# Graph and LSTM kernel on one core: the gates' biases go in through PSUM on ScalarE instead of out through VectorE

## The chip, the cores and the metric

The kernel runs on one core of one Trainium2 chip. The metric is the device time of one execution in microseconds, as a median of several runs.

## The reference

There are 6250 nodes with 512 features and 100000 edges sorted by destination. Two layers follow each other, each with a residual sum:

```python
def gnn(x, edge_index, W1, b1, W2, b2):
    agg = jax.ops.segment_sum(x[src], dst, num_segments=N_NODES)
    h = jax.nn.relu((x + agg) @ W1 + b1)
    return jax.nn.relu(h @ W2 + b2)

def step(carry, x_t):            # LSTM over the 6250 nodes, hidden size 512
    combined = jnp.concatenate((x_t, h_prev), axis=1)
    f, i, o = (sigmoid(combined @ W + b) for f, i, o)
    c_t = f * c_prev + i * jnp.tanh(combined @ W_c + b_c)
    h_t = o * jnp.tanh(c_t)

x = x + gnn(layernorm(x), edges, ...)
x = x + lstm(layernorm(x)[None], ...)[0]
```

## The kernel before

The program has three parts, one after another with a barrier between them. The first (`table_part`) makes the table layernorm(x) @ W1. The second (`graph_part`, the graph stage, where the change is) goes over 50 blocks of 125 nodes. The third (`lstm_part`) solves the recurrence over 125 lanes in rounds of 50 steps; it begins by reading `gate_rows`, which the graph stage has stored, and it runs further rounds only if a check of the values asks for them.

The order of work is written by hand, engine by engine, with semaphores between the engines. In the graph stage one iteration `one(i)` mixes the work of three blocks:

- *Columns of block i.* The edges of a block come as 16 columns of 128 edges (`COLUMNS`), some blocks have more ("beyond"). For each column GpSimd gathers 128 rows of the table by indirect DMA. ScalarE copies them to the rounded fp32r array `high` (`high_part`, L875), VectorE subtracts to get the rest (`low_of_rows`, L1045), and TensorE multiplies both by a one-hot matrix (`visit`, L928) and adds into `agg`. `high` and `low_part` are rings of 8, `onehot` too, and are freed by `s_visit`, in fours.
- *Layers of block i-1.* VectorE adds `agg` to the rows' own table rows (`hin`, L1086), TensorE turns them ("the turn of hin", L943), ScalarE applies bias and relu (L887) and rounds (L892), TensorE multiplies by W2 (`late`, L977 and L981), VectorE adds the bias and the residual and takes the statistics, ScalarE normalises (`z`, L902 to L906), and TensorE turns z ("the turn of z", again L943). ScalarE takes the turned rows as `zT.high` (L910), VectorE the rest as `zT.low` (L1060).
- *Gates.* For each block four PSUM banks `gps` of 512 columns get the products of zT with Wx (L949): `gate_high(n)` is 8 matmuls on zT.high, `gate_low(n)` 4 on zT.low. Banks 1 and 0 of block i-1 are computed at the end of iteration i, banks 3 and 2 of block i-2 during iteration i.
- *Banks out.* VectorE's `gate_biases(b, n)` (L1066) adds the bias row `bgr` to the finished bank and writes `gout`, from where SyncE stores it in `gate_rows`.

"Beyond" columns have a conditional path on every engine: GpSimd's `gather_beyond`, ScalarE's `high_beyond` (L881), VectorE's `beyond_columns` (L1052, L1055) and TensorE's `visit_beyond` (L937), the last between `gate_high(1)` and `gate_high(0)`. ScalarE and VectorE do it at the end of the iteration, ahead of the first columns of the next one. After the last iteration ScalarE alone copies three pieces of weights for the LSTM (L919) before it comes to the barrier.

VectorE and TensorE have two iterations unrolled in a loop; ScalarE has one.

Of the kernel before, what the change touches and what calls it, by code (L numbers as in the profile page):

```python
# [33 lines left out]
ALU = mybir.AluOpType  # L34
ACT = mybir.ActivationFunctionType
# [115 lines left out]
SPREAD = 2 * 16  # L151
# [446 lines left out]
def graph_part(nc, x, edges, table, x1_rows, gate_rows, Wx, W2s, b1c, b2r, bgr, s_w, WEIGHTS_LOADED,  # L598
# [21 lines left out]
    L = LANES  # L620
    BANKS = G4 // PAIR

    with ExitStack() as ctx:
# [70 lines left out]
        s_gps = {n: sem(ctx, f"s_gps{n}") for n in (1, 2)}  # L694
        s_gout = [sem(ctx, f"s_gout{n}") for n in range(BANKS)]
        s_x1_st = sem(ctx, "s_x1_st")
        s_g_st = [sem(ctx, f"s_g_st{n}") for n in range(BANKS)]
# [3 lines left out]
        def wait(e, semaphore, value):  # L701

            if not isinstance(value, int) or value > 0:
                e.wait_ge(semaphore, value)
# [50 lines left out]

        CHECKED = 5
        VISITS = COLUMNS // HOTS

# [112 lines left out]
        def _(e):  # L871
# [11 lines left out]
            def first_layer(i):  # L883
# [5 lines left out]
                for half in range(2):  # L889
                    e.wait_ge(s_relu, i * 4 - (2 - 2 * half))  # L890
                    of = slice(2 * half, 2 * half + 2)
                    e.activation(h1T.high[:, of, :], between_T[:, of, :], ACT.Copy).then_inc(s_h1, 1)  # L892

            def one(i, tiles, layers, gates):
                some, beyond = columns_of(i, high_part, beyond_of(e, high_beyond)) if tiles else (no_columns, no_columns)
                some(0, 8)
                if layers:
                    first_layer(i)
                some(8, 15)
                if layers:  # L900
                    e.wait_ge(s_var, i)
                    e.activation(root[0:L, :], ve[0:L, :], ACT.Sqrt).then_inc(s_norm, 1)  # L902
                    e.activation(z[0:L, :], x1[0:L, :], ACT.Identity, bias=minus[0:L, :]).then_inc(s_norm, 1)
                    e.wait_ge(s_norm, i * 4 - 2)
                    e.wait_ge(s_rs, i)
                    e.activation(z[0:L, :], z[0:L, :], ACT.Copy, scale=rs[0:L, :]).then_inc(s_norm, 1)  # L906
                some(15, 16)
                if layers:
                    e.wait_ge(s_turned, i * 2)
                    e.activation(zT.high[:, :, :], rows_turned[:, :, :], ACT.Copy).then_inc(s_norm, 1)  # L910
                beyond()

            e.wait_ge(s_w, WEIGHTS_LOADED)
            all_iterations(e, one)
            e.wait_ge(s_wh, 16 * WH_LOADS // 2)
# [6 lines left out]
        def _(e):  # L922
# [32 lines left out]
            def gate_high(b, n, agg_done=False):  # L955


                wait(e, s_gout[n], b)
                e.wait_ge(s_norm, (b + 1) * 4)
                products = bank_products(n, zT.high, Wx.high, begins=True)  # L960
                if agg_done:
                    products[0].then_inc(s_agg, 1)
                bank_products(n, zT.high, Wx.low)
# [64 lines left out]
        def _(e):  # L1028
# [33 lines left out]

            def gate_biases(b, n):
                wait(e, s_g_st[n], b * SPREAD)
                e.wait_ge(s_gps[1 if n < 2 else 2], b + 1)
                e.tensor_tensor(gout[0:L, n // 2, n % 2, :], gps[n][0:L, :], bgr[0:L, n, :],  # L1066
                                ALU.add).then_inc(s_gout[n], 1)

            def one(i, par, tiles, layers, gates):
# [23 lines left out]
                lows(8, 10)  # L1093
                if gates:
                    gate_biases(i - 2, 0)
                    gate_biases(i - 2, 1)
                if layers:
# [24 lines left out]
                if layers:  # L1122
                    low_of_turned(zT, rows_turned, i)
                if gates:
                    gate_biases(i - 2, 3)
                    gate_biases(i - 2, 2)
                beyond()
# [976 lines left out]
```

## Time and profile before

| | us |
|---|---|
| median of 3 runs | 2652.29 |
| lowest and highest | 2648.72, 2652.97 |
| the profiled execution, its own time | 2650.73 |
| its span, first to last instruction | 2649.1 |
| graph stage, first column to the barrier | 189 to 1360 |

The profile is of one execution. The span is 1.6 us shorter than that execution's own time. "PE" is TensorE's matmuls, "PEld" its weight loads; a matmul's row is longer than the distance to the next one, since they are pipelined, so a wait is seen better in the weight loads. In a timeline row the first number is the start, the second the length, and the bracket at the end is the idle time before it with the releaser.

### The profile page before, as it was taken

Reading aid. Unit: us, or ns where it says so; the run is one execution under the profiler, and the core shown is the slowest. Engines: PE = TensorE matmul, PEld = TensorE weight load, DVE = VectorE, ACT = ScalarE, POOL = GpSimd, SP = SyncE. Lnnn points to the kernel's source line nnn. Section 1 sums busy time; section 2 is a strip of 40 time slices with the busy share of each in tenths; the row PEclk is TensorE's granted clock in tenths of the full one; section 3 lists DMA queues with packets and bytes.
Section 4 is the critical chain, followed back from the end, with each engine's and each line's share of the span. In section 5 each row is a group of like instructions: output and inputs, shape, how many; then the busy total and the mean of one; then the engine's idle time right before and its main releaser. Section 6 shows DMA issues by size and latency. Waiting matters only on the chain. (4 is left out here: it accounts for less than half of the span.)

```text
span 2649.1 us, 47626 instructions
## 1 busy us (share of the span) xinstructions
PE 2505.1 (95%) x10745; PEld 1819.0 (69%) x10746; DVE 2163.1 (82%) x5780; ACT 1561.6 (59%) x3989; POOL 996.0 (38%) x1017
## 2 busy tenths in 40 slices
PE   7978999999999999999979999999998999989997
PEld 6865777777777777777756666666665555555554
DVE  7757888888888888888848887777777888878887
ACT  5645555555555555555536656666665777757775
POOL 1127777777777767777520000000000000023333
PEclk9987999999999999999989999999999999999999
DMA  9647988888888888888777647777778666589996
GB/s 251 188 132 234 293 281 261 263 279 255 276 265 268 266 244 279 275 255 264 238 195 207 192 124 235 237 240 239 237 235 220 173 172 173 142 224 252 252 251 160
DMA packets 194255, 611.12 MB, mean 231 GB/s; under 512 B 41810, under 2 KB 47954, under 8 KB 164444
## 3 DMA queue, kind: packets, MB, share of 16 engines
q1 hardware_dynamic: 120562, 370.34, 47.1%
q0 software_dynamic: 73632, 240.13, 31.4%
q8 instruction: 19, 0.31, 0.0%
q14 instruction: 42, 0.34, 0.0%
HBM read 468.71 MB, written 141.62 MB: 230 GB/s over the span
## 5 line engine op out<-in xcount | busy, mean ns | idle before, releaser
L834 POOL DMA_INDIRECT kept<-ln_table,kept x800 | 822.3, 1028 | 292.0 <-issue 208.2
L1557 PE MATMUL acc<-shared,state 128*125 128x512 f32 x2244 | 799.3, 429 | 14.4 <-ACT state L1434 13.2
L875 ACT ACTIVATE shared<-kept 128x512 fp32r<-128x512 f32 x800 | 442.6, 625 | 157.3 <-PE agg L928 105.4
L1557 PEld LDWEIGHTS acc<-shared,state 128*125 128x125 f32 x2244 | 413.2, 189 | 153.7 <-ACT acc L1486 27.5
L1391 POOL TENSOR_TENSOR out<-h,lx 125x512 f32<-125x512 f32 x50 | 64.4, 1287 | 1102.2 <-DVE h L1903 1102.2
L928 PE MATMUL agg<-shared,onehot 128*125 128x512 f32 x1200 | 377.6, 408 | 20.7 <-DVE shared L1045 18.6
L1557 PE MATMUL acc<-W_low,state 128*125 128x512 f32 x800 | 316.3, 395 | 0.0
L1557 PE MATMUL acc<-last_high,state 128*125 128x512 f32 x748 | 303.6, 406 | 0.0
L928 PEld LDWEIGHTS agg<-shared,onehot 128*125 128x125 f32 x1200 | 225.2, 189 | 97.9 <-DVE low_part L1045 15.7
L1045 DVE TENSOR_TENSOR low_part<-kept,shared 128x512 fp32r<-128x512 f32 x400 | 265.6, 693 | 11.0 <-ACT shared L875 4.4
L1045 DVE TENSOR_TENSOR shared<-kept,shared 128x512 fp32r<-128x512 f32 x400 | 259.5, 688 | 16.9 <-ACT shared L875 11.1
L949 PE MATMUL gps<-Wx_high,zT_high 128*125 128x512 f32 x800 | 224.2, 402 | 0.8 <-ACT zT_high L910 0.8
L949 PE MATMUL gps<-Wx_low,zT_high 128*125 128x512 f32 x800 | 218.8, 395 | 0.0
L1452 ACT ACTIVATE gate<-acc 125x512 f32<-125x512 f32 x200 | 119.8, 599 | 155.7 <-PE acc L1557 154.9
L949 PE MATMUL gps<-Wx_high,zT_low 128*125 128x512 f32 x800 | 209.6, 394 | 0.0
L1478 ACT ACTIVATE tc<-c 125x128 f32<-125x128 f32 x600 | 153.7, 303 | 77.3 <-DVE c L1895 77.0
L887 ACT ACTIVATE between<-rows_turned,b1c 128x125 f32<-128x125 f32 x200 | 56.7, 367 | 218.3 <-PE rows_turned L943 218.3
L1885 DVE TENSOR_TENSOR c<-gate,c 125x256 f32<-125x256 f32 x300 | 126.4, 421 | 72.0 <-ACT gate L1452 70.2
L949 PEld LDWEIGHTS gps<-Wx_low,zT_high 128*125 128x125 f32 x800 | 149.5, 187 | 37.6
L949 PEld LDWEIGHTS gps<-Wx_high,zT_low 128*125 128x125 f32 x800 | 147.9, 185 | 37.9
L1557 PEld LDWEIGHTS acc<-last_high,state 128*125 128x125 f32 x748 | 138.2, 185 | 50.5 <-DVE state L1878 15.4
L1557 PEld LDWEIGHTS acc<-W_low,state 128*125 128x125 f32 x800 | 150.3, 188 | 30.8
(237 smaller groups left out, 4408.9 us busy)
## 6 DMA issues: line engine op xcount, KB each, us to landing
xg<-total_rows SPq DMA_DIRECT2D x100, 896.0 KB
xg<-gate_rows SPq DMA_DIRECT2D x88, 896.0 KB
gate_rows<-gout SPq DMA_DIRECT2D x200, 224.0 KB
total_rows<-total SPq DMA_DIRECT2D x50, 896.0 KB
kept<-ln_table,kept POOLq DMA_INDIRECT x800, 4.5
lx<-x_rows POOLq DMA_DIRECT2D x50, 250.0 KB, 7.4
out_dram<-out POOLq DMA_DIRECT2D x49, 250.0 KB, 2.8
held<-in_x_dram SPq DMA_DIRECT2D x25, 448.0 KB
```

What stands on the lines that cost most here:

```text
L834: e.indirect_dma_start(out=rows[j % RING][:, :], out_offset=None, in_=table[:, :], in_offset=bass.IndirectOffsetOnAxis(ap=ends[:, b, j, 0: ...
L875: e.activation(high[j % PARTS][:, :], rows[j % RING][:, :], ACT.Copy).then_inc(s_high, 1)
L887: e.activation(between_T[:, m, :], rows_turned[:, m, :], ACT.Relu, bias=b1c[:, m:m + 1]).then_inc(s_relu, 1)
L928: m = e.matmul(sums[0:L, :], onehot[:, j % HOT_RING, :], part[j % PARTS][:, :], start=(j == 0 and part is high), stop=(part is low_part), ...
L949: products.append(e.matmul(gps[n][0:L, :], state[:, k, :], weights[:, k, n // 2, n % 2].rearrange("p s c -> p (s c)"), start=(begins and k ...
L1045: e.tensor_tensor(low_part[j % PARTS][:, :], rows[j % RING][:, :], high[j % PARTS][:, :].bitcast(F32), ALU.subtract).then_inc(s_low, 1)
L1391: e.tensor_tensor(out[par][0:L, :], h[par][0:L].rearrange("c k u -> c (k u)"), x1[par][0:L, :], ALU.add).then_inc(s_out, 1)
L1452: e.activation(gates[0:L, half, 0].rearrange("c s u -> c (s u)"), sums, ACT.Sigmoid).then_inc(s_fi[half], 1)
L1478: e.activation(cell_turned[0:L, k], cell[0:L, k], ACT.Tanh).then_inc(s_tc[k], 1)
L1557: m = e.matmul(acc[n][0:L, :], stationary[:, k, :], weights[k][:, n * PAIR:(n + 1) * PAIR], start=begins, stop=(k == K - 1), skip_group_ch ...
L1885: e.tensor_tensor(half_of(cell, half), gates[0:L, half, 0, 0].rearrange("c (k u) -> c k u", k=KH), half_of(cell, half), ALU.mult).then_inc ...
```

## The change

ScalarE writes each bank's bias into PSUM before the block's products (`seed_bank`), TensorE's first product no longer begins the bank anew (`begins=True` is gone) and adds to what is there, and ScalarE copies the finished bank out (`gate_out`) and seeds it again. VectorE's four sums per block are gone. TensorE now waits for the seed (`s_bias`) where it waited for the bank to be read (`s_gout`).

```diff
+        s_bias = [sem(ctx, f"s_bias{half}") for half in range(2)]
...
+        SEEDED_AS = {1: 1, 0: 2, 3: 1, 2: 2}
...
+            def seed_bank(n):
+                e.activation(gps[n][0:L, :], bgr[0:L, n, :], ACT.Copy).then_inc(s_bias[n // 2], 1)
+
+            def gate_out(b, n):
+                wait(e, s_g_st[n], b * SPREAD)
+                e.wait_ge(s_gps[1 if n < 2 else 2], b + 1)
+                e.activation(gout[0:L, n // 2, n % 2, :], gps[n][0:L, :], ACT.Copy).then_inc(s_gout[n], 1)
+                e.wait_ge(s_gout[n], b + 1)
+                seed_bank(n)
...
-                some(8, 15)
+                some(8, 11)
+                if gates:
+                    gate_out(i - 2, 1)
+                    gate_out(i - 2, 0)
+                some(11, 15)
...
                     e.activation(zT.high[:, :, :], rows_turned[:, :, :], ACT.Copy).then_inc(s_norm, 1)
+                if gates:
+                    gate_out(i - 2, 3)
+                    gate_out(i - 2, 2)
                 beyond()
 
             e.wait_ge(s_w, WEIGHTS_LOADED)
+            for n in (1, 0, 3, 2):
+                seed_bank(n)
...
-                wait(e, s_gout[n], b)
+                e.wait_ge(s_bias[n // 2], b * 2 + SEEDED_AS[n])
                 e.wait_ge(s_norm, (b + 1) * 4)
-                products = bank_products(n, zT.high, Wx.high, begins=True)
+                products = bank_products(n, zT.high, Wx.high)
...
-            def gate_biases(b, n):
-                wait(e, s_g_st[n], b * SPREAD)
-                e.wait_ge(s_gps[1 if n < 2 else 2], b + 1)
-                e.tensor_tensor(gout[0:L, n // 2, n % 2, :], gps[n][0:L, :], bgr[0:L, n, :],
-                                ALU.add).then_inc(s_gout[n], 1)
-
...
                 lows(8, 10)
-                if gates:
-                    gate_biases(i - 2, 0)
-                    gate_biases(i - 2, 1)
                 if layers:
                     e.wait_ge(s_late, i)
...
                     low_of_turned(zT, rows_turned, i)
-                if gates:
-                    gate_biases(i - 2, 3)
-                    gate_biases(i - 2, 2)
                 beyond()
```

Three places show what moves. First, ScalarE at the end of an iteration of the loop, from the last column of a block (`rows15`) over `zT.high` to the conditional path of the beyond column. Before:

```order
L875 ACTIVATE shared<-kept 128x512 [waits s_visit,s_rows15]
L910 ACTIVATE zT_high<-rows_turned 128x500 [waits s_rows_turned]
L739 ISA
L739 TENSOR_LOAD ranges
L768 COMPARE_AND_BRANCH
L751 ISA
```

And now, with line numbers of the changed kernel (its L877 is L875 of before, L926 is L910):

```order
L877 ACTIVATE shared<-kept 128x512 [waits s_visit,s_rows15]
L926 ACTIVATE zT_high<-rows_turned 128x500 [waits s_rows_turned]
L902 ACTIVATE gout<-gps 125x512 [waits s_gps2,s_g_st3]
L897 ACTIVATE gps<-bgr 125x512 [waits s_gout3]
L902 ACTIVATE gout<-gps 125x512 [waits s_gps2,s_g_st2]
L897 ACTIVATE gps<-bgr 125x512 [waits s_gout2]
L740 ISA
L740 TENSOR_LOAD ranges
L770 COMPARE_AND_BRANCH
```

Four instructions stand between `zT.high` and everything that follows: the beyond column and the first columns of the next block. Each seed waits for the copy just ahead of it on the same engine.

Second, VectorE before the change at the same place, between the rest of z and the next block's first one-hot (rows of the beyond path left out behind the first two):

```order
L1045 TENSOR_TENSOR low_part<-kept,shared 128x512 [waits s_high] x3
L1060 TENSOR_TENSOR zT_low<-rows_turned,zT_high 128x500 [waits s_norm]
L1066 TENSOR_TENSOR gout<-gps,bgr 125x512 [waits s_gps2,s_g_st3]
L1066 TENSOR_TENSOR gout<-gps,bgr 125x512 [waits s_gps2,s_g_st2]
L739 TENSOR_LOAD ranges
L768 COMPARE_AND_BRANCH
```

The two L1066 are gone there, and the two that stood ahead of the sum on `late` (L1099) are gone as well; nothing takes their place.

Third, ScalarE at the end of the graph stage. Before, `zT.high` of the last block is followed by the weights' copies:

```order
L906 ACTIVATE between<-between,grs 125x512 [waits s_grs,s_norm]
L910 ACTIVATE zT_high<-rows_turned 128x500 [waits s_rows_turned]
L919 ACTIVATE shared<-kept 128x2048 [waits s_visit,s_wh_rest,s_wh]
L919 ACTIVATE shared<-kept 128x2048 x2
L623 UNCONDITIONAL_BRANCH
```

And now:

```order
L902 ACTIVATE gout<-gps 125x512 [waits s_gps2,s_g_st3]
L897 ACTIVATE gps<-bgr 125x512 [waits s_gout3]
L902 ACTIVATE gout<-gps 125x512 [waits s_gps2,s_g_st2]
L897 ACTIVATE gps<-bgr 125x512 [waits s_gout2]
L940 ACTIVATE shared<-kept 128x2048 [waits s_visit,s_wh_rest,s_wh]
L940 ACTIVATE shared<-kept 128x2048 x2
```

The three copies of the weights now stand behind the last bank's copy, which waits for the last product of the stage.

## Rows read from the trace of the kernel before

**Rows 1.** The page, part 1: TensorE, us, share of the span, instructions.

```profile
PE 2505.1 (95%) x10745; PEld 1819.0 (69%) x10746; DVE 2163.1 (82%) x5780; ACT 1561.6 (59%) x3989; POOL 996.0 (38%) x1017
```

**Rows 2.** Busy time by stretch, 300 to 1300 us: busy us of each engine.

```profile
300.00:1300.00 1000.00, 997.67 (x4418) 777.73 (x4417) 891.52 (x1733) 550.79 (x1152) 738.23 (x719) 1.00 0.86 266
```

**Rows 3.** Waits from 300 to 1300 us: total us, times, longest.

```profile
ACT shared L875 <- PE agg L928: 97.5, 44, 2.2
...
PEld rows_turned L943 <- ACT between L906: 19.4, 44, 0.5
...
PEld agg L928 <- DVE low_part L1045: 11.1, 44, 0.4
DVE between L1099 <- PE late L981: 10.3, 42, 0.3
...
PEld rows_turned L943 <- DVE hin L1086: 6.9, 22, 0.4
```

**Rows 4.** Timeline from 700 us, an even iteration, turn of z to turn of hin.

```profile
709.27 0.41 PEld L943 LDWEIGHTS rows_turned<-ident,between 125*128 125x128 f32 x4 [0.44 <-ACT between L906]
...
709.96 0.59 ACT L910 ACTIVATE zT_high<-rows_turned 128x500 fp32r<-128x500 f32 x1 [0.21 <-PE rows_turned L943]
...
710.58 0.68 DVE L1060 TENSOR_TENSOR zT_low<-rows_turned,zT_high 128x500 fp32r<-128x500 f32 x1
...
710.90 4.28 ACT L875 ACTIVATE shared<-kept 128x512 fp32r<-128x512 f32 x8 [0.36 <-issue]
...
713.65 2.49 DVE L1045 TENSOR_TENSOR shared<-kept,shared 128x512 fp32r<-128x512 f32 x4
...
717.95 0.68 DVE L1086 TENSOR_TENSOR hin<-agg,hin 125x512 f32<-125x512 f32 x1
...
718.82 0.59 PEld L943 LDWEIGHTS rows_turned<-ident,hin 125*128 125x128 f32 x4
```

**Rows 5.** Timeline from 685 us, an odd iteration, same stretch.

```profile
686.54 0.41 PEld L943 LDWEIGHTS rows_turned<-ident,between 125*128 125x128 f32 x4 [0.44 <-ACT between L906]
...
691.34 2.53 DVE L1045 TENSOR_TENSOR shared<-kept,shared 128x512 fp32r<-128x512 f32 x4
...
696.38 0.41 PEld L943 LDWEIGHTS rows_turned<-ident,hin 125*128 125x128 f32 x4 [0.36 <-DVE hin L1086]
```

**Rows 6.** ScalarE's line L881 by source, then a timeline from 409 us, a beyond column.

```profile
L881 ACT ACTIVATE high_x<-rows_x x7: 632/632/635, 416.1 to 1279.1; 128x512 fp32r<-128x512 f32 x7
...
413.99 0.41 PEld L943 LDWEIGHTS rows_turned<-ident,between 125*128 125x128 f32 x4 [0.43 <-ACT between L906]
...
416.07 0.63 ACT L881 ACTIVATE high_x<-rows_x 128x512 fp32r<-128x512 f32 x1 [0.81 <-issue]
...
417.33 0.68 DVE L1055 TENSOR_TENSOR low_x<-rows_x,high_x 128x512 fp32r<-128x512 f32 x1
...
418.16 0.47 PE L937 MATMUL agg<-high_x,onehot_x 128*125 128x512 f32 x1 [0.26 <-DVE low_x L1055]
```

**Rows 7.** Groups by line: count, busy us, mean ns, idle before.

```profile
L1452 ACT ACTIVATE gate<-acc 125x512 f32<-125x512 f32 x200 | 119.8, 599 | 155.7 <-PE acc L1557 154.9
L1486 ACT ACTIVATE acc<-xg 125x512 f32<-125x512 f32 x196 | 116.4, 594 | 0.0
...
L1066 DVE TENSOR_TENSOR gout<-gps,bgr 125x512 f32<-125x512 f32 x176 | 112.5, 680 | 0.0
```

**Rows 8.** Timeline from 1335 us, the end of the graph stage.

```profile
1341.90 5.50 ACT L919 ACTIVATE shared<-kept 128x2048 fp32r<-128x2048 f32 x3
...
1355.19 1.29 DVE L1066 TENSOR_TENSOR gout<-gps,bgr 125x512 f32<-125x512 f32 x2 [4.29 <-PE gps L949]
...
1357.21 0.41 SPq L157 DMA_DIRECT2D gate_rows<-gout  x1
...
1360.17 0.52 POOL L1360 MEMSET total<- 128x512 f16 x1 [29.55 <-POOLq L623]
...
1367.99 2.04 PE L1588 MATMUL acc<-xg,ident_r 125*125 125x512 f32 x4 [12.91 <-DMA xg<-gate_rows]
```

## Prediction

> **What bounds the kernel now.** I read the page first, then the busy time by stretch, then the waits, then two iterations row by row. TensorE is busy 95% of the span [rows 1], and in the steady stretch of the graph stage 997.67 us of 1000, at the full granted clock of 1.00; VectorE has 891.52 there, ScalarE 550.79 [rows 2]. So by busy time ScalarE has room and VectorE is the second fullest engine, but TensorE is the bound. The change takes no matmul away. VectorE's relief is worth only what TensorE waits for VectorE, and ScalarE's new work costs only where TensorE, through some chain, waits for ScalarE. The waits of 44 iterations say how much there is to win [rows 3]: TensorE's weight loads wait 19.4 us for the normalised z, 11.1 us for a `low_part` column and 6.9 us for `hin`, the last in every second iteration. That is 37 us in 44 iterations, 0.85 us of some 22.7 each.
>
> **What VectorE's relief gives.** There are two places.
>
> The sums of banks 0 and 1 stand ahead of the sum on `late`. VectorE waits for TensorE's `late` behind them in 42 of 44 iterations, 10.3 us in all [rows 3]. Taking 2 x 0.68 us [rows 7] from in front of that wait makes the wait longer and nothing earlier. The waits for z and for `low_part` come after it, in a chain that starts at `late` (VectorE's sum, statistics, ScalarE's root, VectorE's scale, ScalarE's z). So 19.4 and 11.1 us stay.
>
> The sums of banks 3 and 2 stand between `zT.low` and the next block's first columns. This is the stretch from the turn of z to the turn of hin. In an even iteration it takes 718.82 - 709.27 = 9.55 us; hin is ready at 717.95 + 0.68 = 718.63, 0.19 us before TensorE wants it, so TensorE's own work makes the 9.55 [rows 4]. In an odd one it takes 696.38 - 686.54 = 9.84 us and TensorE waits 0.36 us, since VectorE's first low column begins at +4.80 instead of +4.38 [rows 5]. The mean is 9.70. Here relief is worth at most 0.29 us in every second iteration.
>
> **What ScalarE's copies cost at that place.** Behind `zT.high` now stand copy, seed, copy, seed. No row shows these two operations on `gps`, but near twins exist: a 125x512 row out of PSUM takes 599 ns, one into PSUM 594 ns, VectorE's sum 680 [rows 7]. Back-to-back rows start closer than they are long: eight columns take 4.28 us [rows 4] where one takes 0.63 (rows 6 show that length for the same shape), so (4.28 - 0.63)/7 = 0.52 apart, an overlap of 0.10. A seed can't overlap the copy it waits for. The nearest handovers are `zT.low` starting at 710.58, 0.01 to 0.03 us after `zT.high` ends at 709.96 + 0.59 [rows 4], and TensorE's beyond product, 0.15 after VectorE's row ends at 418.01 [rows 6]. I take 0.05 for ScalarE's wait on itself. The shift of whatever follows is then
>
> S = 0.49 + 0.60 + 0.05 + 0.49 + 0.60 + 0.05 = 2.3 us.
>
> The time from the last ScalarE row to the next block's first column (710.90 - 709.96 = 0.94, loop and branch) stays, since it is the same code behind the last seed. So `high` 0 starts 1.63 + S after the turn of z [rows 4], ends 0.63 later, and the first low column can start 0.03 after that, at 2.29 + S. From there to the turn of hin it is 696.38 - 691.34 = 5.04 us of VectorE's own work [rows 5]. The stretch becomes the larger of 9.55 and 7.33 + S. With S = 2.3 that is 9.63, in odd and even iterations alike, because VectorE now waits for ScalarE in both and its loop's end is hidden under that. Against 9.70 it is 0.07 us less. Of 49 turns seven have a beyond column and a few at the start wait for gathers, so I count 40: **-3 us**. It is a near tie by arithmetic: 1.36 us off VectorE's chain, 2.3 us onto the one that feeds it.
>
> What hides the other copies: banks 1 and 0 go out behind column 10, and ScalarE idles up to 2.2 us there, 97.5 us in 44 iterations, for TensorE to free the ring before column 12 [rows 3]. With column 11 behind them they end about when that idle time ended. If the cover were short by a few tenths, columns 12 to 14 would be late, and VectorE takes them a microsecond or more after; so nothing. The seeds themselves are ready 7 us or more before TensorE's next product on the bank. SyncE gets banks 1 and 0 about 0.5 us later and has x1's and x's transfers behind them, needed an iteration later. The first four seeds fall in ScalarE's wait for the first gathers. TensorE's products without a new beginning cost what they did.
>
> **Beyond columns.** Seven blocks have one [rows 6]. There ScalarE's `high_x` starts 416.07 - 413.99 = 2.08 us after the turn of z, `low_x` on VectorE at +3.34, TensorE's product at +4.17, and TensorE already waits for it. Behind four more ScalarE rows `high_x` starts at 2.08 + S = 4.38, and `low_x` at 4.38 + 0.63 + 0.03 = 5.04, 1.70 later than now. Here the wait is TensorE's directly and no cover exists; all later work of the block shifts. 7 x 1.70 = **+12 us**.
>
> **The end of the stage.** Before, ScalarE copies the LSTM's weights from 1341.90 for 5.50 us, beside TensorE's last products [rows 8]. Now these copies stand behind the last bank. The last pair starts at 1355.19; 0.60 + 0.05 + 0.49 + 0.60 + 0.05 + 0.49 = 2.28 later, at 1357.47, the copies begin, and they end at 1362.97. The next part had begun by 1360.17, some 2.55 us after the last store was issued (1357.21 + 0.41), and its first matmul waits for a transfer issued after that. So the LSTM begins at least 2.8 us later; I take **+3 us**. The bounds are 0, if the barrier did not wait for ScalarE, and 2.8 + 2.55 = 5.4.
>
> **Sum.** -3 + 12 + 3 = +12 on the profiled execution's 2650.73 gives 2663; the median of the runs is 1.6 higher, so 2664.5, 0.5% slower.
>
> **The unknown cost.** S decides. From below, a wait on itself that costs nothing, not even the overlap, gives 4 x 0.50 = 2.0: the stretch is then TensorE's 9.55, -0.15 x 40 = -6; beyond 7 x 1.40 = +10; end +3; together +7, 2659. From above, with 0.25 for each own wait (rows 6 show 0.15 at another engine), S = 2.7: +0.33 x 40 = +13, 7 x 2.10 = +15, end +5; together +33, 2685. I take 2.3, by the handovers that ScalarE itself gives.
>
> One rule stands against the row. The Trainium skill, Perfetto Trace Analysis, section DVE / Act Engine Instruction, says that a row begins only when the engine executes, after its prefetch, and that a waiting instruction can begin that prefetch only once the semaphore has propagated; so a wait on itself should show a gap of prefetch and propagation. The rows' 0.03 us after `zT.high` speak for a small one. If ScalarE's wait on its own PSUM write costs the 0.25 us of the upper case above, that is the rule's outcome, and the time is 2685.
>
> **The rivals.**
>
> 1. *ScalarE's wait on itself is dear* (S from 2.5 to 2.8): hin is late in every iteration, TensorE waits for it 44 times of 44, 2672 to 2687. For it: 0.10 us more in S is 4 us in the loop and 0.7 beyond. Against: the handover rows. Chance 0.22.
> 2. *No measurable change* (a measurement of this kernel tells about 0.2%, 5 us): S near 2.0 and the barrier not held by ScalarE, +4. Against: three things must be small at once. Chance 0.14.
> 3. *Faster*: the place is VectorE's chain from `late` to z. If the two sums ahead of `late` did hold it up, their 1.36 us would come off the waits for `low_part` and z, at most (19.4 + 11.1)/44 = 0.69 us in 49 iterations, -34, against +12: 2630. It decides as soon as half of the iterations start that chain earlier. Against it: VectorE waited for `late` in 42 of 44. Chance 0.06.
> 4. *The change does something else*: if TensorE's first products overwrote a seed instead of adding to it, the sums in `gate_rows` would be others, and the LSTM, whose rounds depend on values, could ask for one more, (2649 - 1360)/4 = 320 us if its four rounds are alike: 2980. Against it: the LSTM's own 196 seeds go in from ScalarE in the same way [rows 7]. Chance 0.01. The Trainium skill, PSUM — Partial Sum Buffer, section PSUM: the matmul accumulator, has the rule for it: a matmul without a new beginning adds only where TensorE's written bits are set, and a ScalarE write doesn't set them. [...]
>
> The forecast itself (2657 to 2672) has 0.57. Faster by over 0.2%: 0.07; within: 0.15; slower: 0.78. The range 2655 to 2686 leaves out most of rivals 3 and 4 and the lower edge of 2.
>
> **What the profile after would show.** The turn of hin is reached 9.6 us after the turn of z in both kinds of iterations, 7.33 + S if S is larger; VectorE's first low column waits for ScalarE's column, as it never did. VectorE's wait for `late` grows from 0.25 to about 1.6 us, while the waits for z and `low_part` stay at 0.44 and 0.25. TensorE's wait at the beyond product grows by 1.7 us in seven blocks. ScalarE's weight copies start near 1357 plus what the loop has moved, and the next part begins right after their end. ScalarE is at about 76% of the steady stretch, VectorE at 77%. The forecast is wrong if a seed reaches TensorE late, if ScalarE's rows in PSUM are longer than 0.6 us, or if ScalarE comes late to the root and z behind columns 12 to 14.

## The result, and the profile after

The changed kernel takes 2693.49 us (median of 4 runs, 2692.65 to 2694.03); the kernel before, run beside it, 2652.63 us (4 runs, 2648.72 to 2654.49). The ratio is 1.0155, 95% interval 1.0143 to 1.0168. The prediction said 2664.5 in a range of 2655 to 2686. The sign was right. The size was not: 43 us between the two profiled spans, where 12 were expected. In another run of both, the changed kernel took 2693.34 and the ratio was 1.0163 [1.0149, 1.0176].

The first row is the page's line of busy times, the second the busy times from 300 to 1300 us (PE, PEld, DVE, ACT, POOL, then the granted clock), for the changed kernel. They answer to [rows 1] and [rows 2].

```profile
PE 2514.1 (93%) x10745; PEld 1824.4 (68%) x10746; DVE 2055.7 (76%) x5580; ACT 1781.1 (66%) x4393; POOL 1000.6 (37%) x1017
...
300.00:1300.00 1000.00, 973.77 (x4262) 754.60 (x4261) 769.86 (x1506) 717.04 (x1451) 719.84 (x697) 0.99 0.85 259
```

VectorE is at 77% of the steady stretch, as forecast. But TensorE, which was busy for 997.67 us of 1000, now has 973.77: it waits. The waits of the changed kernel in the same stretch (total us, times, longest) say for whom. They answer to [rows 3].

```profile
DVE between L1111 <- PE late L1002: 60.5, 42, 1.5
DVE shared L1066 <- ACT shared L877: 54.0, 37, 1.9
ACT shared L877 <- issue: 35.7, 37, 1.2
...
PEld rows_turned L964 <- DVE hin L1101: 26.3, 38, 1.0
PEld rows_turned L964 <- ACT between L922: 19.0, 43, 0.5
...
PEld agg L958 <- issue: 17.7, 6, 3.1
...
PEld agg L949 <- DVE low_part L1066: 11.3, 45, 0.4
```

The wait for `late` took in VectorE's relief (10.3 us became 60.5), and the waits for z and for `low_part` are what they were (19.4 and 11.1 before). What grew is the wait for `hin`, 26.3 us in 38 iterations where it was 6.9 in 22, and one at the beyond columns, `agg` L958. The first comes from the third row: 37 times ScalarE's first column is preceded by 1 us of "issue", idle time in which the engine waits for no semaphore. The second comes from the same kind of idle time ahead of `high_x`.

One iteration of the changed kernel, from the turn of z to the turn of hin, answers to [rows 4]. Columns are start, duration, engine, line, operation, and in brackets the idle time and what ended it.

```profile
701.44 0.41 PEld L964 LDWEIGHTS rows_turned<-ident,between 125*128 125x128 f32 x4 [0.44 <-ACT between L922]
...
702.13 0.59 ACT L926 ACTIVATE zT_high<-rows_turned 128x500 fp32r<-128x500 f32 x1 [0.22 <-PE rows_turned L964]
...
702.61 0.59 ACT L902 ACTIVATE gout<-gps 125x512 f32<-125x512 f32 x1
...
703.24 0.60 ACT L897 ACTIVATE gps<-bgr 125x512 f32<-125x512 f32 x1
...
703.77 0.58 ACT L902 ACTIVATE gout<-gps 125x512 f32<-125x512 f32 x1
...
704.39 0.60 ACT L897 ACTIVATE gps<-bgr 125x512 f32<-125x512 f32 x1
...
706.20 4.28 ACT L877 ACTIVATE shared<-kept 128x512 fp32r<-128x512 f32 x8 [1.21 <-issue]
...
706.86 2.50 DVE L1066 TENSOR_TENSOR shared<-kept,shared 128x512 fp32r<-128x512 f32 x4 [1.37 <-ACT shared L877]
...
711.17 0.68 DVE L1101 TENSOR_TENSOR hin<-agg,hin 125x512 f32<-125x512 f32 x1
...
711.90 0.42 PEld L964 LDWEIGHTS rows_turned<-ident,hin 125*128 125x128 f32 x4 [0.95 <-DVE hin L1101]
```

The four rows are as forecast: the last seed starts 704.39 - 702.13 = 2.26 us behind `zT.high`, and S was put at 2.3. ScalarE's wait on its own copy costs 703.24 - (702.61 + 0.59) = 0.04. But the column starts 706.20 - 704.39 = 1.81 behind that last row, where before it started 0.94 behind `zT.high`. Nearly all of this 0.87 appears again one step on: the turn of hin comes 711.90 - 701.44 = 10.46 us after the turn of z, and not 9.63.

The trace also says what fills the gap. The view of a tile lists the sequencer's own instructions (a q behind the engine's name), and the code of the branch holds one that is not short: the load of a register from the table `ranges`, from which the branch decides. ScalarE's, from 300 to 1300 us, with least, median and longest ns, in the kernel before and in the changed one:

```profile
L739 ACTq TENSOR_LOAD <-ranges x44: 274/277/285, 301.9 to 1277.8; - x44
```

```profile
L740 ACTq TENSOR_LOAD <-ranges x43: 283/928/1142, 306.8 to 1290.9; - x43
```

The one in the iteration above took 1.14 us, 0.86 more than the usual 0.28. Take the load out of the time from the last row to the next column, and 0.67 us are left in each of the 37 ordinary iterations of either kernel (0.667 to 0.675). So the load is the whole of the growth.

The same stretch with a beyond column answers to [rows 6]:

```profile
418.07 0.41 PEld L964 LDWEIGHTS rows_turned<-ident,between 125*128 125x128 f32 x4 [0.44 <-ACT between L922]
...
421.01 0.60 ACT L897 ACTIVATE gps<-bgr 125x512 f32<-125x512 f32 x1
...
423.22 0.63 ACT L883 ACTIVATE high_x<-rows_x 128x512 fp32r<-128x512 f32 x1 [1.60 <-issue]
...
423.88 0.69 DVE L1076 TENSOR_TENSOR low_x<-rows_x,high_x 128x512 fp32r<-128x512 f32 x1 [2.51 <-ACT high_x L883]
...
424.72 0.71 PE L958 MATMUL agg<-high_x,onehot_x 128*125 128x512 f32 x1 [2.73 <-DVE low_x L1076]
...
425.65 1.91 PE L970 MATMUL gps<-Wx_high,zT_high 128*125 128x512 f32 x4
```

`high_x` starts 5.15 us after the turn of z, where 4.38 was forecast (2.08 before): 2.21 behind the last seed, not the 1.4 that it took behind `zT.high`. The taken path loads from `ranges` twice, here in 0.87 and 0.50 us, before in 0.28 and 0.28. TensorE then waits 2.73 us, and its next four products take 1.91 us where the steady ones take 1.10. The stretches of the changed kernel from 421 us have the granted clock in the third last column. The line below them is the kernel before, around the same product:

```profile
421.00:425.00 4.00, 1.27 (x6) 0.77 (x5) 1.20 (x3) 2.38 (x5) 3.09 (x4) 0.97 1.00 345
425.00:429.00 4.00, 4.00 (x12) 3.08 (x12) 3.38 (x6) 3.04 (x6) 3.08 (x4) 0.60 0.77 257
429.00:433.00 4.00, 4.00 (x20) 3.20 (x19) 3.84 (x7) 0.00 (x0) 3.09 (x4) 1.00 0.73 205
```

```profile
418.00:422.00 4.00, 3.84 (x17) 3.10 (x18) 3.11 (x7) 2.90 (x6) 3.19 (x3) 1.00 0.87 258
```

Behind its idle time TensorE is granted 0.60 for 4 us, so it runs most of them at 1.2 GHz and not at 2.4. The seven iterations with such a column take 27.57, 25.89, 27.14, 27.21, 25.51, 27.26 and 27.39 us (turn of z to turn of z), 26.85 in the mean, where the kernel before has 23.50.

The sum then is: 42 ordinary iterations at 22.99 instead of 22.57 us (the means of the 37 from 300 to 1300 us), +18; seven with a beyond column, 7 x 3.35 = +23; the first turn of z 0.5 later; and the end. The end of the stage in the changed kernel, which answers to [rows 8]:

```profile
1395.99 0.60 ACT L902 ACTIVATE gout<-gps 125x512 f32<-125x512 f32 x1 [3.20 <-PE gps L970]
...
1398.31 5.49 ACT L940 ACTIVATE shared<-kept 128x2048 fp32r<-128x2048 f32 x3
1404.14 0.52 POOL L1369 MEMSET total<- 128x512 f16 x1 [31.19 <-POOLq L623]
...
1411.50 2.04 PE L1597 MATMUL acc<-xg,ident_r 125*125 125x512 f32 x4 [15.60 <-DMA xg<-gate_rows]
```

The last pair of banks starts 1395.99 - 1355.19 = 40.8 us later than before, the first matmul of the LSTM 1411.50 - 1367.99 = 43.5 later, so the end has added 2.7, and all of the loss is in place when the LSTM begins.

### The profile page after: what moved, and what is told of

It is laid out like the page before. It is cut to its first block and busy times, and to the rows that moved or that the text cites. A ratio compares the mean times of both kernels' runs of the same rounds, so it can differ in the third digit from the quotient of the medians.

```text
span 2692.4 us, 47973 instructions
## 1 busy us (share of the span) xinstructions
PE 2514.1 (93%) x10745; PEld 1824.4 (68%) x10746; DVE 2055.7 (76%) x5580; ACT 1781.1 (66%) x4393; POOL 1000.6 (37%) x1017
## 5 line engine op out<-in xcount | busy, mean ns | idle before, releaser
L1566 PEld LDWEIGHTS acc<-shared,state 128*125 128x125 f32 x2244 | 414.4, 189 | 153.4 <-ACT acc L1495 25.9
L877 ACT ACTIVATE shared<-kept 128x512 fp32r<-128x512 f32 x800 | 443.1, 623 | 70.4 <-issue 38.7
L1066 DVE TENSOR_TENSOR shared<-kept,shared 128x512 fp32r<-128x512 f32 x400 | 259.2, 688 | 75.6 <-ACT shared L877 69.8
L1066 DVE TENSOR_TENSOR low_part<-kept,shared 128x512 fp32r<-128x512 f32 x400 | 266.1, 694 | 13.0 <-ACT shared L877 6.6
L970 PEld LDWEIGHTS gps<-Wx_high,zT_high 128*125 128x125 f32 x800 | 146.7, 189 | 34.5 <-issue 1.7
```

The lines of the kernel that those rows point to most:

```text
L877: e.activation(high[j % PARTS][:, :], rows[j % RING][:, :], ACT.Copy).then_inc(s_high, 1)
L970: products.append(e.matmul(gps[n][0:L, :], state[:, k, :], weights[:, k, n // 2, n % 2].rearrange("p s c -> p (s c)"), start=(begins and k ...
L1066: e.tensor_tensor(low_part[j % PARTS][:, :], rows[j % RING][:, :], high[j % PARTS][:, :].bitcast(F32), ALU.subtract).then_inc(s_low, 1)
L1566: m = e.matmul(acc[n][0:L, :], stationary[:, k, :], weights[k][:, n * PAIR:(n + 1) * PAIR], start=begins, stop=(k == K - 1), skip_group_ch ...
```

## The experiments

Theory A: the whole loss comes from the four ScalarE rows between `zT.high` and what follows it in ScalarE's program (the branch to a beyond column, the loop's end, the next columns). Rivals: the seeds or the copies of banks 1 and 0 cost something in another place, or ScalarE as a whole has too much to do.

**The place of the rows, four variants.** *moved* puts the copies and seeds of banks 3 and 2 behind the next block's eighth column:

```diff
                 some(0, 8)
+                if gates_before:
+                    gate_out(i - 3, 3)
+                    gate_out(i - 3, 2)
...
-                if gates:
-                    gate_out(i - 2, 3)
-                    gate_out(i - 2, 2)
                 beyond()
```

> The changed kernel, but banks 3 and 2 go out one place later: behind the eighth column of the next iteration instead of right behind zT.high. Theory A (the cost is ScalarE's four rows between zT.high and the next columns and the beyond column, and nothing else of the change costs): the first column starts 1.63 us after the turn of z again, the turn of hin comes at 9.55 in odd and even iterations, beyond iterations are as before, the end of the stage stays 3 us late: about 2650 us, ratio 0.998 to 1.000. Theory B (seeding and adding in PSUM, or VectorE's or SyncE's new order, costs by itself wherever the copies stand): it stays near 2690.

*beyond_first* only exchanges the branch and the four rows:

```diff
+                beyond()
                 if gates:
                     gate_out(i - 2, 3)
                     gate_out(i - 2, 2)
-                beyond()
```

> The changed kernel, but banks 3 and 2 go out behind the beyond column's work, still ahead of the next columns. Theory A: the seven beyond iterations lose their extra 4 us each (27.2 against 23.5 us), about -22 to -26, while the ordinary ones stay at 23.0 against 22.6: about 2670. Theory C (most of the loss is in the ordinary iterations, and the beyond ones are long for another reason such as the gathers): less than 8 us come back, 2686.

*copies_first* issues both copies and then both seeds, so that no row waits for the row just ahead of it:

```diff
-                    gate_out(i - 2, 3)
-                    gate_out(i - 2, 2)
+                    gates_out(i - 2, (3, 2))
```

> The changed kernel with both copies ahead of both seeds, so that a seed hardly waits for its copy; the four rows start 0.49 apart, 1.97 instead of 2.26 us. Theory A1 (the branch and loop code behind the last seed costs its 0.9 to 1.8 us whatever stands ahead): only 0.3 us per iteration comes back, 47 x 0.3 = 14: about 2680. Theory A2 (ScalarE's wait on itself is what exposes that code): the first column starts at 3.9 us or less behind the turn of z instead of 4.6, and the loop returns to 22.6 us: about 2662.

*only_10* leaves banks 3 and 2 to VectorE's sums, and has ScalarE seed and copy only banks 1 and 0:

```diff
-                if gates:
-                    gate_out(i - 2, 3)
-                    gate_out(i - 2, 2)
                 beyond()
```

> Only banks 1 and 0 are seeded and copied by ScalarE; 3 and 2 are summed by VectorE as before. Theory A: VectorE only waits 1.4 us longer for late and ScalarE's rows lie in its idle time: no change, ratio 0.999 to 1.001. Theory B (seeding costs by itself): half of the loss, about 2673. Theory D (relief ahead of late is worth something): faster, up to 2640.

These four ran first on a chip on which the kernel before takes 2937.78 us, not 2652. Their ratios there were: moved 1.0149 [1.0132, 1.0165], beyond_first 1.0079 [1.0045, 1.0113], copies_first 1.0221 [1.0169, 1.0274], only_10 1.0011 [1.0000, 1.0022]. A repetition (before 2938.57) gave 1.0134 [1.0109, 1.0158], 1.0104 [1.0084, 1.0124], 1.0248 [1.0223, 1.0274] and 1.0005 [0.9991, 1.0019]. Neither speaks on the theory, for on such a chip the iteration has other bounds. The waits of only_10 in the repetition, 300 to 1300 us, and below them those of the same program on a chip with 2650 us:

```profile
DVE between L1117 <- remote: 174.3, 32, 5.9
...
PEld agg L946 <- DVE shared L1066: 116.5, 32, 4.2
...
ACT shared L877 <- remote: 98.5, 31, 4.2
```

```profile
DVE between L1117 <- PE late L1002: 63.3, 44, 1.5
...
ACT shared L877 <- issue: 13.2, 37, 0.4
...
PEld rows_turned L961 <- DVE hin L1107: 7.1, 22, 0.4
```

The engines wait there for several microseconds where the others have long finished, in nearly every iteration. What slows those chips I don't know. The kernel before alone was then run on a third chip:

> The kernel before, unchanged, for its trace on the chip where the experiments run; the first two jobs ran where before takes 2938 us. If that is one of those chips: iterations of the graph stage of about 27 us instead of 22.6, lengthened between the turn of hin and the turn of z by 4 to 5 us, while the stretch from the turn of z to the turn of hin stays at 9.55 and 9.84.

It took 2649.38 (one run), and the changed kernel 2693.34 beside it, the second result quoted above:

> The changed kernel, unchanged, beside the experiments. Theory A: the stretch from the turn of z to the turn of hin is 10.1 to 10.4 us here too, against 9.55 in moved, copies_first and beyond_first; its last seed starts 2.95 us behind the turn of z and the first column 0.9 to 1.8 behind that. Theory A1 (the branch and loop code costs the same behind copies_first's last seed): that gap is 1.11 constant as there. Theory A2: it is longer and uneven. Ratio to before on a 2650 us chip 1.015, on a 2938 us chip 1.01 to 1.02.

Its trace repeats the first: 22.99 us for an ordinary iteration, 10.21 from turn to turn, 0.59 to 1.10 for the load in ordinary iterations, 26.76 for one with a beyond column.

**The same four where the kernel before has 2650.25 us** (27 runs):

> The kernel of moved where before takes 2650 us. Theory A (the four ScalarE rows behind zT.high are the whole cost): turn of hin 9.55 us behind the turn of z in odd and even iterations, so 22.45 each; beyond iterations 23.5 or less; the end of the stage 3 us late: 2640 to 2652, ratio 0.996 to 1.000. Theory B (seeding or banks 1 and 0 cost too): above 1.003.

> The kernel of beyond_first where before takes 2650 us. On the other chips its first column started only 3.63 us behind the turn of z, 0.54 behind the last seed. Theory A then: ordinary iterations 22.45 (the turn of hin at 9.55), beyond iterations 23.5, the end 3 us late: 2645 to 2655, ratio 0.998 to 1.001. Theory C (order of the beyond work does not matter): 1.010 or more.

> The kernel of copies_first where before takes 2650 us. On the other chips its rows took 1.44 and its first column started at 3.24. Theory A: ordinary iterations 22.45, -0.15 x 40 = -6; beyond iterations still 1.5 to 3 us longer, +10 to +20; the end +3: 2657 to 2668, ratio 1.002 to 1.007. Theory B: 1.012 or more.

> The kernel of only_10 where before takes 2650 us. Theory A: nothing, 0.999 to 1.001; iterations 22.45 and 22.7 in turn. Theory B: 1.005 to 1.008.

Measured: moved 2648.99, ratio 1.0000 [0.9990, 1.0009]; beyond_first 2649.83, 0.9997 [0.9987, 1.0006]; copies_first 2663.27, 1.0047 [1.0031, 1.0064]; only_10 2649.49, 0.9997 [0.9987, 1.0006]. Moved and beyond_first have everything else of the change, the seeds, TensorE's waits for them and VectorE's relief, and lose nothing. An exchange of two neighbouring pieces of ScalarE's program is worth 43 us. The first expectation of beyond_first, 2670, missed: it left the ordinary iterations at 23.0 us, and they came back to 22.50. For copies_first, theory A2 holds in the ordinary iterations: the first column starts 3.23 us after the turn of z and they take 22.50. And only_10 says that banks 1 and 0 neither cost nor bring anything: its ordinary iterations take 22.57, as before.

How beyond_first does it is in its timeline from 691 us:

```profile
691.03 0.41 PEld L964 LDWEIGHTS rows_turned<-ident,between 125*128 125x128 f32 x4 [0.45 <-ACT between L922]
...
691.71 0.59 ACT L926 ACTIVATE zT_high<-rows_turned 128x500 fp32r<-128x500 f32 x1 [0.21 <-PE rows_turned L964]
692.33 0.60 ACT L902 ACTIVATE gout<-gps 125x512 f32<-125x512 f32 x1
...
694.11 0.60 ACT L897 ACTIVATE gps<-bgr 125x512 f32<-125x512 f32 x1
694.65 4.26 ACT L877 ACTIVATE shared<-kept 128x512 fp32r<-128x512 f32 x8
695.30 2.50 DVE L1066 TENSOR_TENSOR shared<-kept,shared 128x512 fp32r<-128x512 f32 x4 [0.23 <-ACT shared L877]
```

The branch, not taken here, delays the first copy by 692.33 - 691.71 - 0.48 = 0.14 (0.48 is the spacing without it): the load of `ranges`, 0.27 us from 691.80, runs while `zT.high` does. The column follows the last seed by 0.54, a plain spacing of rows, although the loop's end lies between. So the code that took 0.94 behind `zT.high`, a spacing included, costs 0.14 more than the spacings with the branch first, and took 1.81 with the rows first. The column starts at +3.62 instead of +4.76 and hin is in time.

**What the cost depends on.** Two more variants split the pairs. *half* leaves bank 3's copy and seed behind `zT.high` and moves bank 2's behind the next eighth column:

```diff
                 some(0, 8)
+                if gates_before:
+                    gate_out(i - 3, 2)
...
                 if gates:
                     gate_out(i - 2, 3)
-                    gate_out(i - 2, 2)
                 beyond()
```

> Only bank 3's copy and seed stay behind zT.high; bank 2's pair goes behind the next block's eighth column. So two rows stand there in place of four. Theory A (the code behind the last row is exposed, and its cost grows with what is in front of it): the last seed starts 1.8 us after the turn of z, the gap to the next column is between the 0.94 of before and the 1.3 to 1.8 of the changed kernel, the column comes at +2.8 to +3.1, in time for hin at 9.55; blocks with a beyond column take 24.3 to 25.2 us; in all 2656 to 2663. Theory B (the gap is a property of the order of the code alone, the same 1.3 to 1.8 with two rows): hin stays in time all the same, but high_x begins 3.9 us or more after the turn of z and these blocks take 25.3 us or more, with TensorE's clock falling, 2663 to 2670.

*beyond_between* puts the branch between the two pairs:

```diff
                 if gates:
                     gate_out(i - 2, 3)
+                beyond()
+                if gates:
                     gate_out(i - 2, 2)
-                beyond()
```

> The branch to the beyond column stands between bank 3's pair and bank 2's. Theory A (what the sequencer does between rows is hidden while rows wait for each other): the branch hides behind bank 3's seed as it does with all four rows behind it, the gap behind the last seed is 0.54 to 0.7, the next column comes at 3.5 to 3.7 and hin is in time (9.55); high_x comes about 3.2 to 3.6 after the turn of z, 1.1 to 1.5 later than before, so 7 x 1.2 = 8 us: 2658, with the end's 3 at 2661. Theory B (the branch and the loop's end cost as much wherever they stand, 1.3 us and more): the last seed or the next column is later by that, hin at 9.8 to 10.2, 2672 to 2680.

Beside a kernel before of 2651.93 us (27 runs), half took 2654.64, ratio 1.0010 [1.0000, 1.0019], and beyond_between 2655.75, 1.0013 [1.0004, 1.0022]. Theory A had expected 2656 to 2663 for half and 2658 to 2661 for beyond_between; both come out 1 to 5 us below. In half the column starts at +2.82 as it said, but the gap did not grow with the rows. A beyond column in half:

```profile
415.58 0.41 PEld L973 LDWEIGHTS rows_turned<-ident,between 125*128 125x128 f32 x4 [0.45 <-ACT between L924]
...
417.38 0.60 ACT L897 ACTIVATE gps<-bgr 125x512 f32<-125x512 f32 x1
418.80 0.63 ACT L883 ACTIVATE high_x<-rows_x 128x512 fp32r<-128x512 f32 x1 [0.82 <-issue]
...
420.30 0.47 PE L967 MATMUL agg<-high_x,onehot_x 128*125 128x512 f32 x1 [0.80 <-DVE low_x L1085]
```

`high_x` starts 1.42 behind the seed, the same as behind `zT.high` before, and TensorE waits 0.80, not 2.73. All the variants in numbers, from the starts of rows in 300 to 1300 us (37 or 38 ordinary iterations; the beyond columns are all seven; the loads are those of the view by tile). A start is counted from the turn of z:

| kernel | ScalarE rows between `zT.high` and the branch | last row to next column, us | row ahead of the branch to `high_x`, us | load of `ranges`: starts at / takes, us | second load, taken path: starts at / takes, us | iteration, ordinary / with beyond column, us |
|---|---|---|---|---|---|---|
| before | none | 0.94 to 0.96 | 1.35 to 1.40 | 0.77 / 0.27 to 0.29 | 1.22 / 0.28 to 0.29 | 22.57 / 23.50 |
| moved | none | 1.02 to 1.06 | 1.35 to 1.43 | 0.77 / 0.27 to 0.29 | 1.22 / 0.28 to 0.29 | 22.51 / 23.30 |
| half | copy, seed | 1.01 to 1.06 | 1.35 to 1.42 | 1.88 / 0.27 to 0.29 | 2.33 / 0.28 to 0.29 | 22.51 / 24.04 |
| beyond_between | copy, seed (two rows behind the branch) | 0.53 to 0.54 | 1.35 to 1.41 | 1.88 / 0.27 to 0.29 | 2.33 / 0.28 to 0.30 | 22.52 / 24.04 |
| beyond_first | none (four rows behind the branch) | 0.53 to 0.54 | 1.35 to 1.41 | 0.77 / 0.27 to 0.30 | 1.22 / 0.28 to 0.29 | 22.50 / 23.42 |
| copies_first | copy, copy, seed, seed | 0.58 to 0.59 | 1.25 to 2.00 | 2.37 / 0.27 to 0.29 | 2.82 / 0.53 to 1.25 | 22.50 / 25.69 |
| changed | copy, seed, copy, seed | 0.95 to 1.81 | 1.64 to 2.21 | 3.03 / 0.28 to 1.14 | 3.6 to 4.3 / 0.28 to 0.50 | 22.99 / 26.85 |

The loads show where the time grew. The two rows of them for copies_first are:

```profile
L740 ACTq TENSOR_LOAD <-ranges x44: 273/276/288, 306.2 to 1291.7; - x44
...
L752 ACTq TENSOR_LOAD <-ranges x7: 528/1053/1248, 419.1 to 1292.2; - x7
```

With all four rows ahead of it the first load is as short as ever, and only the second, 0.45 us further on, is long; so the number of rows is not what makes it long. Every load that starts up to 2.37 us after the turn of z takes 0.27 to 0.30 us, in the six kernels that have such loads. Those that start at 2.8 or 3.0 take 0.28 to 1.25, and the later ones of the changed kernel 0.28 to 0.50. It is not a transfer of instructions either: the page counts 60 packets of the two instruction queues in the whole execution of the changed kernel, and 61 before.

Why the load is long at that moment the runs don't settle. In the changed kernel SyncE issues the first two stores of the banks just copied 1.04 and 0.52 us ahead of every one of these loads, in copies_first 0.82 and 0.30 ahead of the long ones; where the load was short, the first store came 0.38 us ahead at most, or behind it. So the stores are one candidate, and whatever else happens 3 us after the turn of z is another. A kernel that holds ScalarE for 2.3 us there without copying anything would tell them apart; it was not run.

A second thing decides how much of the code is seen. In copies_first the last seed waits for a copy that has ended while the first seed runs, so the sequencer goes on to the branch under the seeds, and the column follows the last one by 0.58. It comes 0.98 behind the end of the second copy, about what the code took behind `zT.high`. Where the last row waits for the row just ahead of it, as in half, the code starts only with that row.

**The end of the stage.** *after_tail* is the changed kernel with the copies of the LSTM's weights ahead of the last block's banks; *moved_tail* is moved with the same edit, the version that might beat both kernels:

```diff
+            weights_high()
             one(BLOCKS + 1, False, False, True)
-            e.wait_ge(s_wh, 16 * WH_LOADS // 2)
...
-            for k in range(K - 1):
-                e.activation(shared[:, k * G4:(k + 1) * G4], ...)
```

> The changed kernel with the weights' copies alone put ahead of the last block's banks. Theory: the end's part of the loss was +3 us of 43, so 2690.5 against 2693.4, ratio 1.0150 where the changed kernel has 1.0163 and the part of the loop stays. Rival: part of the loss in the loop depends on it too (another placing of the code in memory): then the stretch from turn of z to turn of hin leaves 9.8 to 10.4 us.

> Banks 3 and 2 are copied and seeded behind the next block's eighth column, and the copies of the LSTM's weights stand ahead of the last block's banks. Theory: the end of the stage was longer by some 3 us because these copies stood behind the last bank; ahead of it they are hidden again, so this is 3 us below the variant with the banks moved alone: 2646 where the kernel before has 2650, ratio 0.998 to 0.999. Rival: the next part waits for something else than ScalarE's copies (the last store, the last bank's row), and nothing changes, ratio 1.000. The first matmul of the LSTM tells: 12.8 us behind the last bank's copy in the kernel before, 15.5 in the changed one.

after_tail took 2692.01, ratio 1.0148 [1.0132, 1.0163] where the changed kernel had 1.0163 [1.0149, 1.0176]: the totals alone don't tell them apart. The traces do. From the last turn of z to the LSTM's first matmul the changed kernel takes 1411.50 - 1383.09 = 28.41 us (28.55 in after_here) and this one 25.48, 2.9 less. Moved and moved_tail differ by as much, 28.38 and 25.59. The two rows of after_tail:

```profile
1385.40 0.41 PEld L973 LDWEIGHTS rows_turned<-ident,between 125*128 125x128 f32 x4 [1.75 <-ACT between L929]
...
1410.88 2.04 PE L1606 MATMUL acc<-xg,ident_r 125*125 125x512 f32 x4 [12.68 <-DMA xg<-gate_rows]
```

moved_tail took 2647.71 (11 runs), ratio 0.9982 [0.9973, 0.9992], the fastest of all and faster than the kernel before by an amount that its interval just parts from nothing. Its stretch from 300 to 1300 us:

```profile
300.00:1300.00 1000.00, 999.17 (x4433) 780.83 (x4432) 796.09 (x1566) 744.76 (x1507) 748.92 (x719) 1.00 0.87 267
```

TensorE is busy 999.17 us of 1000. The change's idea does work once ScalarE's rows stand elsewhere, but the 997.67 before left it 2.3 us per thousand to win there, of which it took 1.5.

## Why the prediction was wrong, point by point

- **The step that failed**: "The time from the last ScalarE row to the next block's first column (710.90 - 709.96 = 0.94, loop and branch) stays, since it is the same code behind the last seed." It was 0.95 to 1.81, 1.57 in the mean. It is the same code, but one instruction of it, the load of a register from `ranges`, took 0.90 us in the mean of the ordinary iterations where it had taken 0.28. The stretch from turn of z to turn of hin, forecast as 7.33 + S = 9.63, is 10.21 in the mean: the formula holds once this 0.6 is added. Its place in the sum was -3 us, and +18 was measured. The near tie by arithmetic was the warning, since past the tie every tenth of a microsecond costs 4 us. I bounded S on both sides, and did not bound this term at all, although no row showed that code behind four rows, and the listing of the change had TENSOR_LOAD as part of it.
- **Beyond columns**: the mechanism was right (TensorE waits directly, nothing covers it), the size was not, 7 x 1.70 against 7 x 3.35. The same loads make up 0.8 of the difference at the column shown (`high_x` at +5.15 instead of +4.38), 0.57 in the mean of the seven. In five of the seven the fall of TensorE's clock comes on top: there 4 us behind the idle time have a granted clock of 0.57 to 0.69 and the iteration takes 27.1 to 27.6 us, in the other two it stays 1.00 and they take 25.9 and 25.5. So of the 23 us some 12 are the forecast, 7 x 0.57 = 4 the loads, and 5 x 1.6 = 8 the clock (27.3 against 25.7 in the mean). The clock stood nowhere in the prediction. With half, where TensorE waits 0.80, they take 24.04, 0.54 more than before, and the code behind the seed costs there what it did.
- **S**: 2.26 measured, 2.3 forecast. The Trainium skill, Perfetto Trace Analysis, section DVE / Act Engine Instruction, would have each own wait show prefetch and propagation; the trace shows 0.03 to 0.04 us at each handover, so the price of 0.25 that went with that rule in the prediction is not seen here. Rival 1 (2672 to 2687) came nearest to the measured time, and its mechanism is still wrong: S is not what it said.
- **VectorE's relief ahead of `late` is worth nothing**: right, 60.5 us of wait for `late` in 42 iterations, z and `low_part` at 0.44 and 0.25 as before. Rival 3 fell with that, and only_10 shows it alone (0.9997).
- **Banks 1 and 0 hide in ScalarE's idle time, and seeds reach TensorE in time**: right; moved and beyond_first have both and lose nothing.
- **The end, +3**: right, 2.7 behind the last pair and 2.9 by after_tail. In the profiled executions only 1.15 us are left of it between the last turn of z and the LSTM (27.26 before, 28.41 after), because the kernel before, and not the changed one, had a fall of the clock in those microseconds (before_here had none, and takes 25.54):

```profile
1343.00:1347.00 4.00, 4.00 (x12) 3.11 (x12) 0.91 (x2) 4.00 (x3) 0.00 (x0) 0.63 0.43 132
```

- **Odd and even alike, VectorE's first low column waits for ScalarE's**: right (37 waits, 54.0 us). ScalarE at 76% of the steady stretch: 72%, in part since fewer iterations fit into it.
- **Rival 4**: TensorE's instructions are as many as before (10745), so there is no further round. No run shows a lost seed. Rival 2 fell with the time.

So of the 43 us: 18 in the ordinary iterations, 23 at the beyond columns, 0.5 at the start, the rest at the end. That all of the loop's share hangs on the place of four rows ahead of a branch is shown by moved and beyond_first, and that the part which the prediction missed is the load of `ranges`, with TensorE's clock behind it, by the traces. Why that load takes up to 1.14 us at its new moment, and 0.28 at the old one, is not shown.

## What to carry to other kernels

An "issue" gap behind an engine's row is a cost of the code that stands there: look up the sequencer's own instructions in it. If one of them loads from memory, its time can change when it comes to stand at another moment of the iteration, so bound it like any other unknown, above all where the new work makes a near tie with TensorE. Put branches and a loop's end ahead of rows that wait for something anyway, and not between the last such row and the one that the other engines need next. And where a change makes TensorE wait longer in one piece, reckon with its next matmuls at the lower clock: here that came behind waits of 1.9 to 2.9 us, though not behind all of them, and never behind the 0.8 of half.

## What the runs showed of the hardware

- A register load from the table `ranges` on ScalarE's sequencer took 0.27 to 0.30 us when it started up to 2.37 us after the turn of z, in the six kernels of the table that have it there, and 0.28 to 1.25 when it started at 2.8 or 3.0 (43 loads of the changed kernel, seven of copies_first). VectorE's and TensorE's loads from the same table stayed at 0.30 to 0.33 in the changed kernel.
- The rest of that code (a branch not taken and a loop's end), counted from the start of the last row, took 0.67 us in the kernel before and in the changed one, 0.74 to 0.78 in moved and half. Where the load ran ahead of the last row's start, the next column followed that row by 0.54 (beyond_first) and 0.58 (copies_first).
- On ScalarE a seed started 0.03 us after the end of the copy out of PSUM that it waited for (200 pairs in the changed kernel).
- TensorE's granted clock fell to 0.57 to 0.69 over 4 us behind five of the seven beyond columns of the changed kernel, whose products had waited 2.5 to 2.7 us, and not behind the other two (2.2 and 2.5). Four matmuls of 128x512 then took 1.91 us, not 1.10. In copies_first it fell behind two of seven, after waits of 1.9 and 2.2 us. After 0.73 to 0.80 us in *half* it stayed at 1.00 all seven times.
- On two chips the same program took 2938 us and not 2650, with single waits of 4 to 12 us, marked remote or issue, whose cause no row shows; the granted clock over the whole execution was 0.94 to 0.95 there and 0.98 elsewhere. There copies_first lost 2.2 to 2.5%, and moved 1.3 to 1.5%, which loses nothing elsewhere. A variant is judged on a chip where the kernel before has its usual time.
